# One layer's wide cross attention on one core: output weights applied to the values once per batch instead of to the attended rows in every step

## The reference, cut to what matters

```python
def _L1_xattn_ref(query, key, value, Wq, bq, Wk, bk, Wv, bv, Wo, bo, ln_gamma, ln_beta):
    residual = query
    q = (query @ Wq + bq).reshape(b, sq, N_HEAD, KEY_DIM)
    k = (key @ Wk + bk).reshape(b, key.shape[1], N_HEAD, KEY_DIM)
    v = (value @ Wv + bv).reshape(b, value.shape[1], N_HEAD, VALUE_DIM)
    scores = jnp.einsum('bqhd,bkhd->bhqk', q, k) / TEMP
    attn = jax.nn.softmax(scores, axis=-1)
    out = jnp.einsum('bhqk,bkhd->bqhd', attn, v).reshape(b, sq, N_HEAD * VALUE_DIM)
    out = out @ Wo + bo + residual
    mu = jnp.mean(out, axis=-1, keepdims=True)
    var = jnp.var(out, axis=-1, keepdims=True)
    return (out - mu) * jax.lax.rsqrt(var + EPS) * ln_gamma + ln_beta
...
x = x + jnp.tanh(g_xattn[1]) * _L1_xattn_ref(_layernorm(x, axis=-1), ctx_1024, ctx_1024, ...)
```

## Time and profile before

| what | value |
|---|---|
| time, median of 3 runs | 1577.11 us (1574.54 to 1578.02) |
| profiled execution: span | 1592.2 us |
| profiled execution: time of its own beside the span | none given |
| busy share of the span | PE 81%, DVE 59%, ACT 45%, POOL 33% |
| weight loads (PEld) | 47% |
| the touched part | about 284 to 606 us of the span |
| PE busy in four of its stretches | 58.86 of 63.93, 60.30 of 66.37, 55.91 of 61.24, 16.88 of 19.13 us |

### The profile page before, as it was taken

How to read it: one execution, slowest core, us unless ns; L and a number is a source line. 1 busy time by engine, 2 the same in 40 slices (tenths; PEclk the granted TensorE clock), 3 DMA queues, 4 the chain that set the end, 5 groups by cost and what they waited for, 6 DMA issues and landing times. The chain is left out here.

```text
span 1592.2 us, 25277 instructions
## 1 busy us (share of the span) xinstructions
PE 1297.0 (81%) x8946; PEld 752.5 (47%) x8946; DVE 946.5 (59%) x2139; ACT 723.1 (45%) x1940; POOL 527.5 (33%) x625
## 2 busy tenths in 40 slices
PE   2799629579989977784997698989887977996998
PEld 2444317345656645463442455656554434442443
DVE  6466621444555655255664688888764875555664
ACT  3354413166656533342543465655755333454222
POOL 2320340525333361333100365656643320000444
PEclk8599859799999997895998799999988996998999
DMA  2444120330000002322000000000000001000000
GB/s 65 127 130 128 40 66 26 72 75 14 1 1 2 1 27 62 89 58 50 9 10 2 1 1 1 1 2 1 1 1 1 1 10 23 10 3 1 7 7 14
DMA packets 66991, 45.30 MB, mean 28 GB/s; under 512 B 17564, under 2 KB 60261, under 8 KB 66869
## 3 DMA queue, kind: packets, MB, share of 16 engines
q1 hardware_dynamic: 61013, 34.48, 8.4%
q0 software_dynamic: 4096, 8.40, 1.9%
q10 hardware_dynamic: 1760, 0.82, 0.3%
HBM read 24.91 MB, written 13.89 MB: 24 GB/s over the span
## 5 line engine op out<-in xcount | busy, mean ns | idle before, releaser
L3411 ACT ACTIVATE L2a_pr<-psum,L2a_negmax 128x512 f32<-128x512 f32 (+3 forms) x256 | 132.6, 532 | 94.0 <-DVE L2a_negmax L3537 40.1
L557 ACT ACTIVATE L1x_praw<-psum,L1x_negmax 128x154 f32<-128x154 f32 x256 | 96.5, 392 | 78.4 <-DVE L1x_negmax L649 78.2
L318 POOL TENSOR_TENSOR L1x_pm<-L1x_praw,L1x_total 128x1024 f32<-128x1024 f32 x32 | 60.7, 1898 | 160.6 <-DVE L1x_total L655 111.7
L3276 PE MATMUL psum<-ident,L2a_pr 128*128 128x128 f32 x640 | 85.9, 278 | 19.0 <-DVE L2a_pT L3550 11.7
L649 DVE TENSOR_REDUCE L1x_negmax<-psum 128x4 f32<-128x616 f32 x64 | 50.7, 794 | 55.2 <-PE psum L370 51.0
L3276 PEld LDWEIGHTS psum<-ident,L2a_pr 128*128 128x128 f32 x640 | 71.7, 143 | 24.7 <-issue 21.1
L1978 POOL TENSOR_TENSOR L3f_scaled<-L3f_sg,L3f_wide 128x512 f32<-128x512 f32 (+1 forms) x44 | 55.7, 1271 | 66.9 <-ACT L3f_sg L2057 37.9
L1611 DVE TENSOR_REDUCE L3x_negmax<-psum 128x6 f32<-128x924 f32 (+1 forms) x48 | 47.7, 1011 | 46.8 <-PE psum L1149 37.4
L1611 DVE TENSOR_REDUCE L0x_negmax<-psum 128x6 f32<-128x924 f32 (+1 forms) x48 | 47.8, 1010 | 44.9 <-PE psum L1149 40.6
L3161 POOL TENSOR_TENSOR L2a_pr<-L2a_pr,L2a_total 128x1024 f32<-128x1024 f32 x29 | 56.5, 1947 | 46.5 <-DVE L2a_total L3566 46.3
L3164 POOL TENSOR_TENSOR L2a_pr<-L2a_pr,L2a_total 128x768 f32<-128x768 f32 x32 | 48.7, 1520 | 70.0 <-DVE L2a_total L3566 69.7
(11 more groups left out here) (741 smaller groups left out, 3372.1 us busy)
## 6 DMA issues: line engine op xcount, KB each, us to landing
expert_arena<-in_L_ffn_w SPq DMA_DIRECT2D x16, 256.0 KB, 4.4
group_in<-zero SPq DMA_DIRECT2D x2, 1472.0 KB, 9.3
L1f_xs<-group_in SPq DMA_DIRECT2D x10, 256.0 KB, 3.8
group_out<-L1f_ys SPq DMA_DIRECT2D x10, 256.0 KB, 3.6
L1f_gu<-in_L_ffn_gate_up_w SPq DMA_DIRECT2D x8, 256.0 KB, 3.5
slots_in<-zero SPq DMA_DIRECT2D x1, 1280.0 KB, 9.0
L0f_xs<-slots_in SPq DMA_DIRECT2D x5, 256.0 KB, 3.6
resid<-in_x SPq DMA_DIRECT2D x4, 256.0 KB, 5.8
```

What stands on the lines that cost most here:

```text
L318: nc.gpsimd.tensor_tensor(pm[:, n % 2].rearrange("p j t k -> p (j t) k"), praw[:, n % 3, :, :, 0:MAIN].rearrange("p j t k -> p (j t) k"), ...
L557: nc.scalar.activation(praw[:, n % 3, j, t, :], psum[:, 2 * u + j, x * CTX:(x + 1) * CTX], ACT.Exp, bias=negmax[:, n % 2, u, j, x:x + 1], ...
L3276: last = nc.tensor.transpose(psum[:, TURN + n // 4, n % 4 * P:(n % 4 + 1) * P], pr[:, m % RING, n * P:(n + 1) * P], core.ident[:])
L3411: ins = nc.scalar.activation(pr[:, i % RING, SEQ * j + lo:SEQ * j + hi], psum[:, bank + j, lo:hi], ACT.Exp, bias=negmax[:, i % RING, e:e + ...
```

## The change

- **Values times output weights, once per batch.** `values_turned` (3 calls a batch, L358) makes the transposed values of two heads, 160 columns each (the 154 context rows with padding); ACT copies them to `vT`, spare room in another buffer. `values_out` (4 calls a batch, two steps' heads each) multiplies them by their rows of `Wo`: 4 matmuls with 64 rows for the main context rows (L372) and 4 that put out 32 rows for the tails (L374), into H0 and H1; DVE copies them to `vw` (L638, 512 columns) and `vwt` (L642, two copies of 64 x 128). `value`, `vm` and `vt` are gone.
- **Probabilities stationary.** `values(n - 4)` is now 8 matmuls with a 128 x 128 tile of `pT` stationary and `vw` (128 columns) moving (L419), straight into OUT, added up over heads and steps; in odd steps 4 more with `tT` and `vwt` for the tails of two steps (L424). `output`, `oT`, bank OV and ACT's copy are gone; the loop has one pass less.
- **Own bank for queries.** `query` and `rowsT` have bank 6 (now IN) to themselves and don't wait for DVE's `pT` copies; `turned` no longer waits for ACT's query copies. `keys` goes to H0, `values_turned` to H1.
- **Waits for `tT`.** PE waits for the `tT` copy right after `tails` only in steps where H1 is used next (`g` 3 and 5 while a batch follows, `g` 1 from batch 1 on).
- **The end of a batch.** `finished` has four parts: the read of OUT (L672) at `g == 4`, between the `pT` copies and the second maxima, the statistics at the end of that step, the old parts 1 and 2 at `g` 6 and 7. The wait for L672 now stands ahead of `values` of the next batch's first step, on PE at `g == 4`. ACT's square root moves to `g == 5`, and that of the fourth batch's rows to `n == 14`.
- **Ahead of the loop** PE makes `values_turned` and `values_out` of batch 0 in place of the values of batches 0 and 1; the loop starts after 4 queries are copied instead of 8.

The core of the diff:

```diff
-    H0, H1, OV, OUT = 4, 5, 6, 7
+    H0, H1, IN, OUT = 4, 5, 6, 7
...
-                def value(b, i, bank):
-                    rows = core.ctxT[:, b * CTX:b * CTX + MAIN] if i < 2 else core.ctxt[:, b].rearrange("p j k -> p (j k)")
-                    nc.tensor.matmul(psum[:, bank, :], rows, w["wv"][:, (i % 2) * 512:(i % 2 + 1) * 512], start=True, stop=True).then_inc(s["v_ps"], 1)
+                def values_turned(b, i, bank):
+                    g0, g1 = key_unit(i)
+                    for g in range(g0, g1):
+                        last = nc.tensor.matmul(psum[:, bank, (g - g0) * KP:(g - g0 + 1) * KP], w["wv"][:, g * P:(g + 1) * P], core.ctxp[:, b, :],
+                                                start=True, stop=True)
+                    last.then_inc(s["vt_ps"], 1)
+                def values_out(b, i, bank):
+                    pe.wait_ge(s["vt"], 3 * b + (2 * i + 1) // 3 + 1)
+                    for part in (0, 1):
+                        for x in range(2):
+                            g = 2 * i + x
+                            for j in range(G):
+                                rows, k = slice(DK * j, DK * j + DK), 2 * j + x
+                                wo = w["wo"][rows, g * P:(g + 1) * P]
+                                if part == 0:
+                                    last = nc.tensor.matmul(psum[:, bank + j, x * D:(x + 1) * D], vT[rows, g, 0:MAIN], wo, start=True, stop=True)
+                                else:
+                                    last = nc.tensor.matmul(psum[32 * k:32 * k + 32, bank + j, 2 * D:3 * D], vT[rows, g, MAIN:KP], wo, start=True, stop=True)
+                    last.then_inc(s["vw_ps"], 1)
...
                     pe.wait_ge(s["pt"], 2 * m + 2)
-                    pe.wait_ge(s["tt"], m // 2 + 1)
-                    if m:
-                        pe.wait_ge(s["o"], m)
-                    for j in range(G):
-                        h = G * g + j
-                        nc.tensor.matmul(psum[DK * j:DK * j + DK, OV, :], vm[:, b % 2, h * DK:(h + 1) * DK], pT[:, m % 3, j, :], start=True, stop=True)
-                    nc.tensor.matmul(psum[:, OV, :], vt[:, b % 2, g * P:(g + 1) * P], tT[:], start=False, stop=True, skip_group_check=True).then_inc(s["pv"], 1)
+                    pe.wait_ge(s["vw"], 4 * b + g // 2 + 1)
                     if g == 0 and b:
                         pe.wait_ge(s["yr"], b)
-                    for t in range(QT):
-                        last = nc.tensor.matmul(psum[:, OUT, t * P:(t + 1) * P], oT[:, m % 2, t * P:(t + 1) * P], w["wo"][:, g * P:(g + 1) * P],
+                    for j in range(G):
+                        for t in range(QT):
+                            last = nc.tensor.matmul(psum[:, OUT, t * P:(t + 1) * P], pT[:, m % 3, j, t * P:(t + 1) * P], vw[:, b % 2, g, j, :],
...
+                    if g % 2:
+                        pe.wait_ge(s["tt"], m // 2 + 1)
+                        for t in range(QT):
+                            last = nc.tensor.matmul(psum[:, OUT, t * P:(t + 1) * P], tT[:, t * P:(t + 1) * P], vwt[:, b % 2, g // 2, :],
...
-                pe.wait_ge(s["q"], NG)
+                pe.wait_ge(s["q"], 4)
...
+                        if follows and g in (3, 6):
+                            pe.wait_ge(s["k"], 3 * (b + 1) + (1 if g == 3 else 2))
+                        if n < NS and b and g == 0:
+                            pe.wait_ge(s["k"], 3 * (b + 1))
+                        if follows and g in (3, 4, 6):
+                            pe.wait_ge(s["vt"], 3 * (b + 1) + (3, 4, 6).index(g) + 1)
+                        if follows and g in (5, 7):
+                            pe.wait_ge(s["vw"], 4 * (b + 1) + (5, 7).index(g) + 1)
+                        if n < NS and b and g in (1, 2):
+                            pe.wait_ge(s["vw"], 4 * b + 2 + g)
...
-                        if n >= 3 and n % 2:
-                            pe.wait_ge(s["tt"], (n - 1) // 2)
-                                value(b + 1, g // 2 - 2, H1)
+                            keys(b + 1, (2, 5, 7).index(g), H0)
+                        if n >= 3 and n % 2 and (follows and g in (3, 5) or b and g == 1):
+                            pe.wait_ge(s["tt"], (n - 1) // 2)
+                        if follows and g in (2, 3, 5):
+                            values_turned(b + 1, (2, 3, 5).index(g), H1)
+                        if follows and g in (4, 6):
+                            values_out(b + 1, g // 2 - 2, H0)
+                        if b and g in (0, 1):
+                            values_out(b, 2 + g, H0)
-                    if 0 <= n - 5 < NS:
-                        output(n - 5)
...
+                def values_out(b, i, bank):
+                    dve.wait_ge(s["vw_ps"], 4 * b + i + 1)
+                    nc.vector.tensor_copy(vw[:, b % 2, 2 * i:2 * i + 2].rearrange("p x j d -> p j x d"),
+                                          psum[:, bank:bank + 2, 0:2 * D].rearrange("p j (x d) -> p j x d", d=D))
+                    for j in range(G):
+                        rows = slice(2 * 32 * j, 2 * 32 * j + 64)
+                        ins = nc.vector.tensor_copy(vwt[rows, b % 2, i, :], psum[rows, bank + j, 2 * D:3 * D])
...
+                    if b and b < B and g == 4:
+                        finished(b - 1, 0)
                     if n < NS:
                         maxima(n, 1)
```

More of the change, by code:

```diff
@@ L425, in _ @@
                     keys(0, i, i)
-                for i in range(4):
-                    value(0, i, 3 + i)
+                for i in range(3):
+                    values_turned(0, i, 3 + i)
                 for g in range(NG):
@@ L577, in _ @@
                 rows_root(1)
-                for n in range(NS + 5):
+                for n in range(NS):
                     b, g = n // NG, n % NG
@@ L705, in _ @@
                 normed(1)
-                for n in range(NS + 5):
+                for n in range(NS + 4):
                     b, g = n // NG, n % NG
```

183 lines of the change are left out of this document (72 added, 111 removed).

## The result

The changed kernel is slower: median 1589.87 us of four runs (1588.41 to 1592.50), against 1575.82 us for the kernel before, measured with it; ratio 1.0089, 95% interval 1.0074 to 1.0104. The forecast was 1572 us, the range 1558 to 1586.

What follows compares the result with a forecast made beforehand. TensorE's order was taken to set the time, with VectorE next in the last batch. Work, waits, clock and both ends summed to -5.1 us; with the 15.1 us profile-to-median difference carried over, this gave 1572 us, range 1558 to 1586.

Steps and rivals of the forecast that it cites:

- tails: TensorE's waits for the copy of turned tails: eight waits of 0.86 us go, -6.9 us.
- turn-around: Transposes wait for VectorE's copies behind each `values_out`: 0.5 us in 12 places, +6.0 us, between +2.4 and +10.
- L672: `values` of a batch's first step waits for the read of OUT at steps 12, 20, 28: +7.1 us together.
- the last batch: From step 24 on, where VectorE's chain sets the pace, TensorE's shorter step is given back: +3 us, 0 to +5.
- the -8.9: Net TensorE work: 92.7 us added less 101.6 us removed, -8.9 us.
- Rival D: Slower `values_out` turn-around: 32-row matmuls not beside each other, copies at upper bound, +10.8 us, 1583 us; chance 0.23.
- The clock: Last batch: half-clock work behind an idle 0.83 us would hide in the wait for L672, -3.1 us.
- The term of -2.5 behind the loop: Less TensorE work behind GpSimd's last division, if L672 follows PE: -2.5 us, between 0 and -4.1.
- Ahead of the loop: Less PE and copy work before the loop, so `summed` may start earlier: -2 us, between 0 and -4.6.
- B: Waits for VectorE's copies and L672 cost half, and more of the prologue's gain comes: 1564 us; chance 0.17.
- C: The ends don't move: prologue tied to the DMA, L672 to the last scatter, last batch +5: 1578 us; chance 0.16.
- Rival E: Weight loads in the open: each pass pays its load, `values` 4.8 instead of 1.85 us, 1670 us; chance 0.02.

Runs made afterwards that it cites:

- the run on the kernel before: Kernel before, with TensorE waiting for the turned tails' copy only where their bank is used next (six of 14 waits removed): 1570.67 us, ratio 0.9973.
- The run with early scatters: Changed kernel with the first 4 of GpSimd's 16 last-batch scatters one step earlier, behind the third-last step's division: 1586.07 us, ratio 1.0071.
- the tidied change: Changed kernel with late values, values ahead of transposes, early scatters, more waits removed, unused matmuls in waits and ahead of the loop: 1565.56 us, ratio 0.9935.
- the second trace of the kernel before: Kernel before, unchanged, profiled once more: 1578.38 us, span 1576.6.

## Why the prediction was wrong

- **Waits: right as a sum.** Inside the loop (added up over the rows of the timeline) TensorE idles 36.4 us in place of 25.4, +11.0; the terms for tails, turn-around, ScalarE, L672 and the last batch made -6.9 + 6.0 + 2.2 + 7.1 + 3.0 = +11.4. One by one: L672 7.4 (3.73, 1.15, 2.49), but the kernel before had 1.8 of waiting for L672 and the query in their place, so +5.5 for +7.1; the turn-around 0.63 in 11 places, +7.0 for +6.0; the tail waits gone where said, -5.6 in the loop for -6.9, which the run on the kernel before bears out; the rest +4.1 for +5.2. That the sum is nearer than its terms is luck.
- **TensorE's work: a term mis-sized by some 3.7 us.** Busy time in the loop rose by 1.3 us; without the slow clock (next point, +2.9) the work fell by 1.6, where the -8.9 has 5.3 of its 32 steps' saving inside the loop. `values` 1.89 us (1.85 costed) and the tails 0.89 to 0.98 (0.95) were right, the 32-row matmuls 0.35 (0.40). But `values_turned` cost 2.65 a batch instead of 2.3 (0.91, 0.99 and 0.75), the main part of the product 0.65 instead of 0.55, and scores and queries that now stand beside another form cost 0.05 to 0.1 more. Rival D's ground is thus there in small (1.0 instead of 0.95 us, 0.63 instead of 0.5 of waiting), far below the +0.45 a place at which it was to decide.
- **The clock: a step that failed.** "After the change PE stands behind L672 at that place, so that such a stretch hides in the wait: -3.1." The opposite came: waits of 2 to 3.7 us, three of them made or lengthened by the change, are each followed by a stretch at half the clock. Counted from the rows (work behind the wait less the same work elsewhere), steps 12, 16, 27 and 28 lose 1.6, 1.1, 1.6 and 1.7 us, 6.0 in all, where the kernel before loses 1.5 and 1.6 at two places: about +2.9 instead of -3.1, 6.0 us of the miss. The unused matmuls at steps 16 and 27 show idleness in such a wait as a cause, not only as a pattern. Not every wait is followed by one, nor only the long ones: the kernel before has its slow stretches behind 0.83 and 1.47 us, and none behind 2.60 us at step 16.
- **The end: the other step that failed, counted twice and then reversed.** The term of -2.5 behind the loop (out of -4.1) is the shorter work of the last values, which the -8.9 of all 32 steps already held (3.6 of it). And "if L672 follows PE" was right, but the sum has TensorE's shorter work behind a last division that stays where it was, and that division came later: the second-last one starts 4.9 us behind the last step's first scores instead of 1.9 (569.17 to 574.03, and 558.93 to 560.84), and the four scatters put the last one 8 us behind it, as before. Steps 29 and 30 got 3.0 us shorter (15.5 to 12.5), and VectorE did not follow: from 564.13 to 580.5 its rows show no wait. ScalarE has the sums of step 30 ready at 571.00, VectorE inverts them only at 573.76, behind the second part of the batch's end (now at `g` 6) and the router's table:

```profile
573.76 0.19 DVE L655 RECIPROCAL L1x_total<-L1x_total 128x8 f32<-128x8 f32 x1
```

  So "Parts 1 to 3 move, at the same cost on VectorE" was not free here. The outcome: 4.47 us of waiting in place of 1.03, with half clock behind it (+1.5), +1.0 instead of -6.1. The run with early scatters takes 3.1 us of this back in the attention's part, 1.4 up to the next layer; no run moved VectorE's part, so its share is read from one trace and not shown.
- **Ahead of the loop:** -0.5 instead of -2.0. The 2.12 us stall that the bounds rested on was that one execution's.

Together: 6.0 + 3.7 - 0.4 in the loop, 7.1 behind it, 1.5 ahead of it, some 18 us from -5.1 to the +12.9 of the attention's part. The rivals missed it: B and C were about the size of terms, D about the wrong place. Rival E (whose 16 x 0.31 is 4.96, not 4.8) is refuted: 16 passes with 16 loads of 204 ns (L419) take 1.89 us, 0.12 a pass. The Trainium skill's sentence that a weight load overlaps matmuls in flight only where the row groups differ (TensorE: Matmul & The Clock Gate, "What overlaps and what doesn't") doesn't describe this trace. The Trainium skill's rule that a change of the tiling mode drains TensorE (TensorEngine Tiling (Array Packing), Key Properties) agrees with the trace, at about 0.1 us: the query takes 0.86 us ahead of transposes (427.20 to 428.06) and 0.96 ahead of the product's 64-row form (434.57 to 435.53).

Is the new form of the values worth anything? With most of the waits and slow stretches of both taken out, the times are level (1565.6 and 1564.6). It is not a clean test of the two forms: the tidied change keeps a slow stretch in the loop (some 1.5 us) and another behind it, its `summed` comes a step earlier than in the other, and its attention's part, 2.7 us shorter in the profile (296.9 and 299.6), reaches the next layer's first matmul only 0.8 us earlier, since that layer waits for the scatters. Whether it would win without these no run shows. Its saving of TensorE work in the loop is small, the 1.6 us above, and the new waits cost more.

## What to carry to other kernels

Cost a new wait on TensorE with what the clock may do behind it: here waits of 2.0 to 3.7 us cost another 1.1 to 1.7 us of half-speed work, and unused matmuls at step 16 gave that back in a stretch of the same length. When one engine gets faster, read what is queued on the others ahead of the work that it will ask for sooner; here four scatters stood in front of the last division, and VectorE's own queue in front of the one before. And compare two profiled executions only together with their times: a span 16 us above the median made a stall of one execution look like part of the kernel.

## What the runs showed that was not expected

- The same stretch of 3.64 us is followed by work at 0.61 or at 1.00 of the clock, depending only on two unused matmuls (2.0 us) in it. Not every idle stretch is followed by slow work: step 16 of the second trace of the kernel before has 2.60 us of it, and its query behind takes the usual 0.96 us.
- That same wait in the kernel before without tail waits is 2.61 us, and there slow work does follow (the query 1.84 us). Each is one execution; in these two, an edit that only moved a wait in time came with a slow stretch elsewhere.
